# The value bias as a GpSimd addition in a staging buffer in place of a thirteenth product per value unit

## The reference

```python
x_in = _ln(x, lnkv_g, lnkv_b)          # x is the context, (4, 1024, 512)
k = x_in @ wk + bk
v = x_in @ wv + bv
slots = q_mu + jnp.exp(q_logsig) * noise   # noise is the normalised input
for _ in range(T):                      # T = 3
    prev = slots
    q = _ln(slots, lnq_g, lnq_b) @ wq + bq
    logits = jnp.einsum('bnd,bkd->bnk', k, q) / scale
    attn = jax.nn.softmax(logits, axis=-1) + EPS_ATTN
    attn = attn / jnp.sum(attn, axis=1, keepdims=True)
    upd = jnp.einsum('bnk,bnd->bkd', attn, v)
    ...
```

## Time and profile before

| | |
|---|---|
| median of 3 runs | 2357.03 us (2356.34 to 2360.32) |
| profiled execution | 2363.11 us, its span 2361.4 us |
| TensorE busy | 2312.7 us, 98% of the span |
| VectorE busy | 1605.5 us, 68% |
| ScalarE busy | 975.1 us, 41% |
| GpSimd busy | 993.7 us, 42% |
| mean granted TensorE clock | 0.99 |

### The profile page before, as it was taken

One profiled execution on the slowest core, in us unless ns is written; L12 is line 12 of the kernel. 1 busy time (PEld: TensorE's weight loads), 2 busy tenths in 40 slices (PEclk: granted clock), 3 DMA queues, 4 the chain that ended last, 5 costly groups with the idle time before them and its releaser, 6 DMA issues.

```text
span 2361.4 us, 30933 instructions
## 1 busy us (share of the span) xinstructions
PE 2312.7 (98%) x11557; PEld 1900.6 (80%) x11557; DVE 1605.5 (68%) x2915; ACT 975.1 (41%) x1646; POOL 993.7 (42%) x1345
## 2 busy tenths in 40 slices
PE   8999999999999999999999999999999998999998
PEld 4888888888878888887888888888888887777886
DVE  7777657757477575768757567785775769965542
ACT  2566443343333333333333433334333345756432
POOL 1576235151453515435354452544535157733200
PEclk9999999999999999999999999999999999989999
DMA  5587000000052000013400001350000012204330
GB/s 201 198 312 252 1 1 1 1 1 19 32 193 75 1 23 5 14 50 138 139 6 19 9 10 54 115 162 5 10 19 1 19 55 80 91 10 131 106 112 18
DMA packets 87125, 158.58 MB, mean 67 GB/s; under 512 B 10801, under 2 KB 33337, under 8 KB 83134
## 3 DMA queue, kind: packets, MB, share of 16 engines
q1 hardware_dynamic: 82838, 150.26, 18.5%
q0 software_dynamic: 2688, 6.31, 0.9%
q10 hardware_dynamic: 1450, 0.04, 0.0%
HBM read 106.21 MB, written 50.37 MB: 66 GB/s over the span
## 4 chain that ended last, share of the span: by engine, by line
PE 79%; DVE 12%; POOL 4%; ACT 2%; issue 2%; DMA 0%; ACTq 0%; DVEq 0%; POOLq 0%
PE ps L221 24%; PE ps L223 24%; PE ps L222 24%; PE ps L1501 3%; DVE moments L2002 3%; POOL gT1l L2621 2%; DVE slots L2401 2%; DVE tbuf L2395 1%; DVE zTl L2043 1%; DVE tbuf L2388 1%; PE ps L1657 1%; DVE mx L2348 1%; ACT prob L1905 1%; PE ps L447 1%; PE ps L1486 1%
## 5 line engine op out<-in xcount | busy, mean ns | idle before, releaser
L221 PE MATMUL ps<-zTh,kTl 128*128 128x512 f32 (+1 forms) x912 | 334.1, 366 | 10.6 <-DVE zTl L2043 8.0
L223 PE MATMUL ps<-zTh,kTh 128*128 128x512 f32 (+1 forms) x912 | 326.3, 358 | 0.0
L222 PE MATMUL ps<-zTl,kTh 128*128 128x512 f32 (+1 forms) x912 | 326.2, 358 | 0.0
L221 PE MATMUL ps<-vh,prob_lo 128*128 128x512 f32 x768 | 306.1, 399 | 0.0
L223 PE MATMUL ps<-vh,prob_hi 128*128 128x512 f32 x768 | 300.1, 391 | 0.0
L222 PE MATMUL ps<-vl,prob_hi 128*128 128x512 f32 x768 | 299.3, 390 | 0.0
L2043 DVE TENSOR_TENSOR zTl<-ps,zTh 128x512 fp32r<-128x512 f32 x224 | 151.2, 684 | 200.4 <-ACT zTh L1770 200.4
L2519 POOL TENSOR_SCALAR rs_m<-mv_m 128x1 f32<-128x1 f32 x96 | 55.3, 576 | 544.4 <-DVE mv_m L2004 542.7
L1905 ACT ACTIVATE prob<-ps,nb 128x1024 f32<-128x1024 f32 x96 | 107.2, 1117 | 256.5 <-DVE nb L2353 256.0
L221 PEld LDWEIGHTS ps<-zTh,kTl 128*128 128x128 f32 x912 | 173.0, 190 | 44.1 <-DVE zTl L2043 15.7
L1752 ACT ACTIVATE zbuf<-slots,rs_m 128x512 f32<-128x512 f32 x96 | 78.4, 816 | 303.4 <-POOL rs_m L2524 303.4
(11 more groups left out here) (331 smaller groups left out, 5744.1 us busy)
## 6 DMA issues: line engine op xcount, KB each, us to landing
ctx<-in_ctx_dram SPq DMA_DIRECT2D x8, 1024.0 KB, 7.5
slots<-in_x_dram SPq DMA_DIRECT2D x8, 1024.0 KB, 6.7
kT_d<-kTh SPq DMA_DIRECT2D x6, 1024.0 KB, 7.7
kT_d<-kTl SPq DMA_DIRECT2D x6, 1024.0 KB, 9.6
s_d<-slots SPq DMA_DIRECT2D x6, 1024.0 KB, 5.1
v_d<-vh SPq DMA_DIRECT2D x6, 1024.0 KB, 9.6
v_d<-vl SPq DMA_DIRECT2D x6, 1024.0 KB, 11.6
kTh<-kT_d SPq DMA_DIRECT2D x3, 2048.0 KB, 10.6
```

What stands on the lines that cost most here:

```text
L221: nc.tensor.matmul(out, ll, rh, start=start, stop=False)
L222: nc.tensor.matmul(out, lh, rl, start=False, stop=False)
L223: return nc.tensor.matmul(out, lh, rh, start=False, stop=stop)
```

## The change

The thirteenth matmul, its operands and `value_bias` go. A value unit now takes four steps: `kv_raw` (ScalarE) copies the bank to one of three staging buffers (the two halves of `gbuf` and the second half of `tbuf`), `add_bias` (GpSimd) adds `rows[:, 2, :]` in place, `kv_hi` (ScalarE) rounds the buffer to `vh`, and `kv_lo` (VectorE) subtracts the two, both from SBUF. The bank is free after `kv_raw`. All three engines' programs are reordered for this; the main lines:

```diff
+    kv_buf = [gbuf[:, 0, :], gbuf[:, 1, :], tbuf[:, 1, :]]
+    KV_BUF = (0, 1, 0, 1, 2, 0, 1, 2)
+    KV_AGO = (3, 3, 2, 2, 5, 3, 3, 3)
...
-                    if u >= 4:
-                        pe.wait_ge(sem("row_step"), 3 * (C + 1) + 5)
-                        last = nc.tensor.matmul(bank(n % 6), two[:, :], vb_row[:, :], start=False, stop=True)
...
+            def kv_raw(h, u):
+
+                n = 8 * h + u
+                act.wait_ge(sem("kv_done"), n + 1)
+                if n >= KV_AGO[u]:
+                    act.wait_ge(sem("kv_lo"), n - KV_AGO[u] + 1)
...
+                    A.activation(kv_buf[KV_BUF[u]], bank(n % 6), ACT.Copy).then_inc(sem("kv_read"), 1)
...
+                else:
+                    act.wait_ge(sem("v_added"), 4 * h + u - 3)
+                    A.activation(v[0][:, 4 * nh + u - 4, :], kv_buf[KV_BUF[u]], ACT.Copy).then_inc(sem("kv_hi"), 1)
...
             for h in range(1, HS - 1):
                 c_norm(h + 1, 0); c_norm(h + 1, 1)
+                kv_hi(h - 1, 7)
                 kv_hi(h, 0)
...
-                kv_hi(h, 6)
+                kv_raw(h, 6); kv_hi(h, 5)
                 x_norm(h, 3)
-                kv_hi(h, 7)
+                kv_raw(h, 7); kv_hi(h, 6)
...
-                V.tensor_tensor(lo, gbuf[:, u % 2, :] if u < 4 else bank(n % 6), hi.bitcast(f32), ALU.subtract)\
-                    .then_inc(sem("kv_lo"), 1)
+                V.tensor_tensor(lo, kv_buf[KV_BUF[u]], hi.bitcast(f32), ALU.subtract).then_inc(sem("kv_lo"), 1)
...
+            def add_bias(h, u):
+
+                n = 8 * h + u
+                pool.wait_ge(sem("kv_read"), n + 1)
+                G.tensor_tensor(kv_buf[KV_BUF[u]], kv_buf[KV_BUF[u]], rows[:, 2, :], ALU.add).then_inc(sem("v_added"), 1)
...
-                first_slots(h, 0)
-                first_slots(h, 1); first_slots(h, 2)
+                first_slots(h, 0); first_slots(h, 1)
+                if h == HS - 1:
+                    first_slots(h, 2); first_slots(h, 3)
+                    add_bias(h, 4); add_bias(h, 5)
+                    rstd_z0(h)
+                    add_bias(h, 6); add_bias(h, 7)
+                    continue
+                add_bias(h, 4)
+                first_slots(h, 2)
+                add_bias(h, 5)
                 if h + 2 < HS:
                     rstd_c(h + 2)
+                add_bias(h, 6); add_bias(h, 7)
                 first_slots(h, 3)
                 if 1 <= h <= C:
                     scale_w1(h - 1)
-            rstd_z0(HS - 1)
```

More of the change, by code:

```diff
@@ L2136, in _ @@
             kv_lo(0, 2)
-            value_bias()
             fold(6)
@@ L2157, in _ @@
                 x_stats(h, 0); x_stats(h, 1)
+                kv_lo(h - 1, 7)
                 if h == 1:
@@ L2200, in _ @@
             z_lo(0, 0)
-            kv_lo(h, 4)
+            z0_stats(h, 0)
             z_lo(0, 1)
-            z0_stats(h, 0); z0_stats(h, 1)
-            kv_lo(h, 5)
+            z0_stats(h, 1)
             z_lo(0, 2)
             z0_stats(h, 2); z0_stats(h, 3)
+            kv_lo(h, 4)
+            z_lo(0, 3)
+            kv_lo(h, 5)
             kv_lo(h, 6)
-            z_lo(0, 3)
             kv_lo(h, 7)
```

91 lines of the change are left out of this document (34 added, 57 removed).

## The result

| | before | after |
|---|---|---|
| median of 4 runs each, same chip | 2358.68 us (2356.34 to 2360.37) | 2381.85 us (2380.93 to 2383.82) |
| ratio, 95% interval | | 1.0096 (1.0084 to 1.0108) |
| profiled execution | 2363.11 us | 2381.49 us |
| TensorE / VectorE / ScalarE / GpSimd busy | 2312.7 / 1605.5 / 975.1 / 993.7 us | 2317.5 / 1617.8 / 992.6 / 1042.7 us |

The change costs 23.2 us between the medians and 18.4 us between the two profiled executions. 2371.7 was predicted, at most 2379. The sign was right, the size was not. How narrowly depends on the figure: the range ended 22 us above the kernel before, between the two gaps of the medians and above that of the profiles.

A forecast was written before the change was run, and what follows sets the result against it. The prediction took TensorE alone to set the value phase's pace. It summed -7.25 + 2.1 (block 2) + 4 x 3.3 (blocks 3 to 6) + 6.6 (block 7, first logits) = +14.7 us, from 2357.03 to 2371.7; range 2361 to 2379.

The forecast's parts named there:

- The matmul's price: TensorE, value phase: 32 matmuls fewer at 0.227 us each gain 7.25 us, 0.91 per block.
- the chain of 15.7 us on GpSimd: Each block: three first slots, three additions and `rstd_c(h + 2)` take 15.7 us together, so unit 6's addition ends at 24.4.
- the wait of 2.1: TensorE waits 2.1 us for the next block's first transposes, ready at 25.8 and due at 23.7; blocks 2 to 6.
- block 1 without a wait of its own: Block 1 is spared: GpSimd's 3.80 us of idling before `rstd_c(2)` takes in the two additions there.
- additions of 1.32 us on average: GpSimd's four bias additions per block: 1.37 us each at the lower end, 1.7 at the upper.
- stretched neighbours: VectorE instructions with two SBUF inputs and GpSimd's SBUF-reading ones lengthen each other; `vl` subtractions go from 0.66 to 1 to 1.8 us.
- three waits in block 7: Block 7 and ahead of the first logits: TensorE waits 1.15, 3.2 and 2.3 us, together 6.6.
- what would show it: Signs listed for the changed profile: TensorE waits, longer periods, GpSimd over 21 us busy per block, stretched subtractions, unchanged slot rounds.
- TensorE's clock: Last sentence: the forecast is wrong if the clock falls in the waits and they cost more than they last; no price.
- the w1 chunk: Blocks 2 to 5: GpSimd's chunk holds VectorE's subtraction and delays `rstd_x`, so the next wait is 3.3 us, not 2.1.
- The rivals: Additions don't meet VectorE: 2357.4 us, 9%; TensorE stays the bound: 2350, 8%; VectorE becomes the bound too: 2379, 13%.
- VectorE becomes the bound too: Rival, 13%: value subtractions of up to 1.58 us bring VectorE to 22.3 busy; blocks lose 1.5 us more: +22, 2379.

The follow-up runs named there:

- the two experiments: The changed kernel with one matmul per value unit issued twice, its first result overwritten (2373.98 us), and filled (2374.28 us).
- filled: The changed kernel with eight unread matmuls issued on TensorE in the wait ahead of the first transposes, in blocks 2 to 6; 2374.28 us.
- before_twelve: The kernel before without its thirteenth matmul, the bias left out; 2352.8 us.
- after_again: The changed kernel itself, measured once more in another batch; 2379.94 us, 18.8 us above the kernel before.
- stats_first: The changed kernel with ScalarE's `c_norm` ahead of unit 6's rounding and VectorE's moments of the next input rows ahead of unit 6's subtraction; 2370.93 us.
- stats_chunks: stats_first with the four w1 chunks moved behind GpSimd's value phase; 2372.33 us.

## Why the prediction failed, step by step

I set the profiled executions side by side, by the first transposes of blocks 1 and 6 and by those of z row 4 (before: 85.94, 208.94, 258.14; after: 86.67, 220.85, 277.08; block 6 of before is 184.34 and one period).

| stretch | predicted | measured |
|---|---|---|
| to block 1 | -0.9 | +0.7 |
| blocks 1 to 5 | +10.8 | +11.2 |
| block 6 to z row 4 | +4.8 | +7.0 |
| sum | +14.7 | +18.9 |

**Right.** The matmul's price; the chain of 15.7 us on GpSimd and the wait of 2.1, step by step, on ScalarE's `zc`; block 1 without a wait of its own; additions of 1.32 us on average and stretched neighbours; three waits in block 7, with their lengths. These I named as what would show it, and it did.

**Wrong, and the step that failed: TensorE's clock was costed at nothing.** It stood in the last sentence as something that would make me wrong, and had no price, no rival and no part of the range. In after it is low six times: at block 1, behind four of the five waits at a block's transposes, and behind that of the first logits. The four cost 5.9 us (1.5 each for the three inside blocks 1 to 5, 1.4 for the one in block 6), and the two experiments took out 5.6. The one at block 1 costs 1.6 us but isn't tied to the change (below), and that behind the first logits costs nothing up to z row 4 (below).

**Wrong, and hidden in the sum: the w1 chunk.** "The wait is then 3.3 us" was 4 x 1.2 = 4.8 us too much. The waits are 1.97 to 2.07. The path I drew from the chunk over the moments to `rstd_x` exists, but I had let the chunk hold VectorE's first subtraction of a key until 5.45. In filled, with the clock at 1.00, that subtraction took 0.68 us beside the chunk and ended 4.1 us after the transposes (142.66 + 0.68); it was GpSimd's instruction that stretched, to 2.53 us. `rs_x` came 8.05 us after the transposes and not 9.1. In blocks 1 to 5 this error (+4.8) and the clock (4.5) cancel, with 0.7 us left over, so the right sum there is no merit.

**Right by its waits: block 7.** 1.15, 3.2 and 2.3 us were predicted, 6.6 in all. In filled, where the clock stays at 1.00 behind the first logits, they are 1.10 and these:

```profile
267.00 0.50 PE L219 MATMUL ps<-zTh,kTl 128*128 128x512 f32 x1 [3.54 <-DVE zTl L2055]
272.06 1.11 PE L1503 MATMUL ps<-ident,zbuf 128*128 128x128 f32 x4 [2.03 <-ACT zbuf L1812]
```

In after they are 0.98, 3.57 and 0.68. From the first logits to z row 4 it is 5.05 us there (272.03 to 277.08) and 5.06 in filled, so the low clock in after took its time out of the third wait and moved nothing. Of the 2.2 us more than predicted in this stretch, 1.4 are block 6's low clock (56.2 against 54.8 in the two experiments); 0.8 I can't ascribe.

**Block 1.** Its transposes come 1.6 us late. 32 one-column matmuls stand ahead of it in both kernels, and in after the clock is low behind them. It is low there in 14 of the 15 profiles of kernels that issue them in one piece, those of before_twelve and after_again among them; the profile of before is the exception. So this part belongs to the execution more than to the change.

**The medians** differ by 23.2 and 18.8 us in two batches, the profiles by 18.4. The stretch from L389 to the end (last section) takes one of two times, 4 us apart, whatever the kernel. Both profiles of the first batch have the longer one, so 18.4 is free of it. A median of a few runs can move by it; whether it did so here isn't shown, since the other runs have no trace.

**The rivals.** "VectorE becomes the bound too" gave 2379, the closest, by the wrong mechanism: VectorE is busy 20.7 us of a block, and no wait of TensorE in blocks 2 to 6 of after goes back to it. In stats_first and stats_chunks one does.

## What to carry to other kernels

A wait on TensorE can have a price beside its length. Where a stretch that kept TensorE busy gets a wait of about 2 us, give a chance and a price to the matmuls behind it running at half the clock, and ask whose start stands behind these. Here that was 1.4 to 1.6 us where the next chain hung on them, and nothing where another wait took it up. A filler of unread matmuls is a quick test of it, and in filled the value phase was shorter with it than with idling.

An engine with a third of its time free isn't free for work in a chain. Four additions took GpSimd from 16.4 us of a block of 24.6 to 23.4 us and more of a block of 25.9 to 27.5; they are 5.3 us of this, the rest is neighbours that got longer. Moving the place where TensorE waited did not bring the mean block under 25.6 us in any order tried. The addition on the engine that subtracted from the bank before (VectorE, 0.68 us against 1.32) needs one hand-over fewer than ScalarE's copy and GpSimd's addition, and reached 23.69 us a block, but only after two reorderings.

When terms of opposite sign agree with the total, test each one alone before believing any.
